# Half of the cross keys kept as differences from the other half: a decoder layer on one NeuronCore

## What is computed

```python
# part 1: linear attention with 16 heads of 64 (relu features)
# part 2, both attentions with 16 heads of 16:
q, k, v = heads(x @ Wq + bq), heads(x @ Wk + bk), heads(x @ Wv + bv)
y = softmax(causal(q @ k.T * scale)) @ v
qc = heads(x @ Wcq + bcq)
kc = heads(context @ Wck + bck)          # 1024 keys
vc = heads(context @ Wcv + bcv)
y = y + softmax(qc @ kc.T * scale) @ vc
x = layernorm(x + y @ Wp + bp)
# part 3: each row goes to the best of 8 experts (256 -> 1024 -> 256)
```

## Time and profile before

| | us |
|---|---|
| median of 3 runs | 2289.46 (2287.99 to 2290.59) |
| the profiled execution | 2287.69 |
| its span in the trace | 2286.0 |
| granted TensorE clock, mean | 0.994 of full speed |

### The profile page before, as it was taken

One profiled execution on the slowest core, in us unless ns is written; L12 is line 12 of the kernel. 1 busy time (PEld: TensorE's weight loads), 2 busy tenths in 40 slices (PEclk: granted clock), 3 DMA queues, 4 the chain that ended last, 5 costly groups with the idle time before them and its releaser, 6 DMA issues. The chain is left out here.

```text
span 2286.0 us, 51067 instructions
## 1 busy us (share of the span) xinstructions
PE 2169.5 (95%) x16290; PEld 1352.2 (59%) x16291; DVE 1366.7 (60%) x3905; ACT 1102.2 (48%) x1680; POOL 367.5 (16%) x628
## 2 busy tenths in 40 slices
PE   8999999999899999999999999999999899799998
PEld 4555554556455555555555645554555455499997
DVE  2588357844785458635883478357844685255554
ACT  1267524761477227732674257524762377233332
POOL 1011111111111111111111111111111111122222
PEclk9999999999999999999999999999999999899999
DMA  7440025102520162005300350026102520655553
GB/s 235 155 164 25 2 106 200 48 2 85 198 71 2 47 234 73 2 11 189 130 25 9 141 180 25 1 97 209 48 2 85 198 71 2 221 181 182 183 182 109
DMA packets 115763, 235.75 MB, mean 103 GB/s; under 512 B 19614, under 2 KB 42655, under 8 KB 113344
## 3 DMA queue, kind: packets, MB, share of 16 engines
q1 hardware_dynamic: 112112, 224.23, 29.3%
q0 software_dynamic: 3408, 8.41, 1.0%
HBM read 154.04 MB, written 73.17 MB: 99 GB/s over the span
## 5 line engine op out<-in xcount | busy, mean ns | idle before, releaser
L1201 ACT ACTIVATE es<-ps 128x1024 f32<-128x1024 f32 (+1 forms) x704 | 665.3, 984 | 250.7 <-PE ps L809 181.4
L1412 DVE TENSOR_REDUCE craw<-ps 128x1 f32<-128x512 f32 x1024 | 636.7, 684 | 115.0 <-PE ps L773 115.0
L773 PE MATMUL ps<-hk,hq 64*128 64x512 f32 x1024 | 391.4, 450 | 24.7 <-DVE craw L1412 8.6
L807 PE MATMUL ps<-hq,hk 64*128 64x512 f32 x1024 | 325.0, 440 | 2.2 <-ACT es L1201 2.2
L1408 DVE CUSTOM_DVE_ANT_0 ps<-ps,causal 128x512 f32<-128x512 f32 (+3 forms) x512 | 236.2, 518 | 91.4 <-PE ps L770 91.0
L773 PEld LDWEIGHTS ps<-hk,hq 64*128 64x128 f32 x1024 | 174.7, 184 | 194.8 <-DVE craw L1412 129.3
L809 PE MATMUL ps<-mrow,minus 64*128 64x512 f32 x1024 | 285.8, 391 | 0.0
L837 PE MATMUL ps<-es,vca 128*17 128x256 f32 x4096 | 276.6, 382 | 1.2 <-ACT es L1201 0.3
L661 POOL TENSOR_SCALAR_AFFINE_SELECT es<-es 128x256 f32<-128x256 f32 x256 | 99.0, 406 | 659.5 <-ACT es L1201 659.4
L1731 ACT ACTIVATE hT<-ph,b1s 128x128 f32<-128x128 f32 x312 | 89.2, 369 | 182.8 <-PE ph L1694 182.8
L809 PEld LDWEIGHTS ps<-mrow,minus 64*128 64x128 f32 x1024 | 166.0, 186 | 10.1
(11 more groups left out here) (210 smaller groups left out, 2838.3 us busy)
## 6 DMA issues: line engine op xcount, KB each, us to landing
w1s<-in_w1T SPq DMA_DIRECT2D x39, 1024.0 KB, 5.4
hk<-scr_kc SPq DMA_DIRECT2D x64, 512.0 KB, 5.1
scr_kc<-staged SPq DMA_DIRECT2D x16, 1024.0 KB, 4.3
scr_qc<-staged SPq DMA_DIRECT2D x32, 512.0 KB, 4.5
scr_q<-staged SPq DMA_DIRECT2D x32, 512.0 KB, 5.3
hq<-scr_qc SPq DMA_DIRECT2D x56, 256.0 KB, 4.4
hq<-scr_q SPq DMA_DIRECT2D x56, 256.0 KB, 4.2
hk<-scr_k SPq DMA_DIRECT2D x56, 256.0 KB, 4.6
```

The source lines that it names most:

```text
L773: last = mm(pb, hq[i][at, T + t * P:T + (t + 1) * P], hk[i][at, T + half * BANK:T + (half + 1) * BANK], start=True, stop=True)
L807: mm(pb[a], hk[i][rows[a], T + j * P:T + (j + 1) * P], hq[i][rows[a], T:2 * T], start=True, stop=False)
L1201: nc.scalar.activation(es[:, k % ERING, :].rearrange("p (a c) -> p a c", a=HB)[:, :, 0:w], eslot[k % 2][:].rearrange("p (a c) -> p a c", a ...
L1412: last = v.reduce_max(craw[p % 2][:, t, a:a + 1, 1 + half], pb, AX.X)
```

## The change

The cross keys of the context's first 512 positions are no longer kept; what stands in their place is their difference from the keys of the last 512 (key i less key i + 512). GpSimd takes the difference of the context itself (context_difference, into a part of es), kcprod multiplies it, and the bias falls out of it. Scores of the first half are then scores of the second half plus the product with the difference, and that product is added onto the bank where the scores of the second half stand:

- exponentials: a unit of the second half is 4 products as before. The unit of the first half two units later goes to the same PSUM tensor, which still holds scores less maximum, and adds 2 products of differences. No maximum is added again.
- maxima: the product for the first half ("rest") is added onto the bank of the second half's, once VectorE has reduced that one. Count and size of products and reductions are the same.

Places in PSUM are worked out anew (places): pair 0 uses four banks for its maxima (zbank is free then), later pairs have bank 1 for the first head and banks 0 and 2 in turn for the second head, the rows and the turned results. The order of maxima (max_of) and of exponential units (UNITS) is by parity of the pair. A step is now: weigh two, 1 maximum, unit k, 1 maximum, unit k+1, 2 maxima (and a row at that border). AHEAD goes from 8 to 12, the first groups from 3 to 4.

```diff
-AHEAD = 8
-ROW_AFTER = (4, 6)
+AHEAD = 12
+ROW_AFTER = (8, 6)
+def cross_tile(c):
+    i = c // 4 * 2 + c % 2
+    return (i, True) if c % 4 >= 2 else (NTC // 2 + i, False)
+OWN_UNITS = [("own", i, False) for i in range(NSELF)]
+CROSS_UNITS = [("cross", *cross_tile(c)) for c in range(NTC)]
+UNITS = (OWN_UNITS + CROSS_UNITS, OWN_UNITS[:2] + CROSS_UNITS + OWN_UNITS[2:])
+SELF_MAX = [("self", i, False) for i in range(len(MAX_SELF))]
+BY_TILE = [("cross", t, rest) for t in range(NT) for rest in (False, True)]
+BY_TWO = [("cross", 2 * n + t, rest) for n in range(NT // 2) for rest in (False, True) for t in range(2)]
+def max_of(p, m):
+    n, a = divmod(m, HB)
+    cross = BY_TWO if a or p == 0 else BY_TILE
+    return (*(cross + SELF_MAX if p % 2 or p == 0 else SELF_MAX + cross)[n], a)
-FIRST_PARTS = [("v", 1, 3), ("qc1", 0, 3), ("q1", 0, 3), ("k1", 0, 3),
+FIRST_PARTS = [("v", 1, 4), ("qc1", 0, 4), ("q1", 0, 4), ("k1", 0, 4),
                ("qf0", 0, 4), ("qf0", 1, 4), ("qf1", 0, 4), ("qf1", 1, 4)]
...
-        order += take(HB)
+        order += take(1)
         if k + 1 < steps:
             order.append(("exp", *divmod(k + 1, NU)))
-        order += take(1)
+        order += take(HB, True)
...
+def places():
+    place, former, last, count = {}, {}, {}, [0, 0]
+    for e in RING:
+        kind, p, m = e
+        if kind == "max" and m % HB == 0:
+            at = (1, 3)[count[0] % 2] if p == 0 else 1
+            count[0] += 1
+        else:
+            at = (0, 2)[count[1] % 2]
+            count[1] += 1
+        place[e], former[e], last[at] = at, last.get(at), e
...
+    return place, former
...
-        eslot = [ps[2], ps[3]]
+        eslot = [ps[3], ps[2]]
...
+            def context_difference():
+                nc.gpsimd.tensor_tensor(ctxd_s, ctxT_s[:, 0:TC_ // 2], ctxT_s[:, TC_ // 2:TC_],
+                                        ALU.subtract).then_inc(s_ctxd, 1)
...
                 first_sum()
+                pool.wait_ge(s_ctx, (b + 2) * 16)
+                context_difference()
                 pool.wait_ge(s_route, b + 1)
...
-                n = RING_AT[entry]
-                if n >= MBANKS:
-                    kind, p, _ = former = RING[n - MBANKS]
+                former = SAME[entry]
+                if former is not None:
+                    kind, p, _ = former
...
-                    last = mm(pb, hq[i][at, T + t * P:T + (t + 1) * P],
-                              hk[i][at, T + half * BANK:T + (half + 1) * BANK], start=True, stop=True)
+                    keys = hk[i][at, T:T + BANK] if rest else hk[i][at, T + BANK:T + TC_]
+                    last = mm(pb, hq[i][at, T + t * P:T + (t + 1) * P], keys, start=not rest, stop=True, skip_group_check=rest)
...
-                if k == 0:
-                    pe.wait_ge(s_act, cur(b, N_ACT, ACT_AT["qf1"]))
+                if k < 2:
+                    pe.wait_ge(s_act, cur(b, N_ACT, ACT_AT[("qf0", "qf1")[k]]))
...
-                turned = range(HB - 1, -1, -1)
+                turned = (0, 1) if k % 2 else (1, 0)
...
                     for a in turned:
-                        mm(pb[a], hk[i][rows[a], T + j * P:T + (j + 1) * P], hq[i][rows[a], T:2 * T], start=True, stop=False)
-                    for a in turned:
-                        last = mm(pb[a], neg[a], mrow[p % 2][rows[a], :], start=False, stop=True)
+                        last = mm(pb[a], hk[i][rows[a], T + j * P:T + (j + 1) * P], hq[i][rows[a], T:2 * T],
+                                  start=not rest, stop=rest, skip_group_check=rest)
+                    if not rest:
+                        for a in turned:
+                            last = mm(pb[a], neg[a], mrow[p % 2][rows[a], :], start=False, stop=True)
...
-                                      ctxT_s[:, half * 512:(half + 1) * 512], start=True, stop=True)
+                                      ctxT_s[:, 512:TC_] if half else ctxd_s, start=True, stop=True)
...
-                    high = nc.scalar.activation(stage[:, stg, 0, at:at + w], t[:, 0:w], ACT.Identity,
+                    skip = TC_ // 2 if w == TC_ else 0
+                    if skip:
+                        nc.scalar.activation(stage[:, stg, 0, at:at + skip], t[:, 0:skip], ACT.Copy)
+                    high = nc.scalar.activation(stage[:, stg, 0, at + skip:at + w], t[:, skip:w], ACT.Identity,
                                                 bias=bias_c[:, bias_n, m:m + 1])
...
-                    for c in range(0, w, 512):
+                    skip = TC_ // 2 if w == TC_ else 0
+                    if skip:
+                        v.tensor_tensor(stage[:, stg, 1, at:at + skip], t[:, 0:skip], stage[:, stg, 0, at:at + skip].bitcast(F32),
+                                        ALU.subtract)
+                    for c in range(skip, w, 512):
```

More of the change, by code:

```diff
@@ L130, in heads_order, with take @@
         maxima.insert(at, ("row", p, 0))
-    def take(count):
+    def take(count, border=False):
         taken = []
-        while maxima and (count or maxima[0][0] == "row"):
+        while maxima and (count or border and maxima[0][0] == "row"):
             count -= maxima[0][0] == "max"
@@ L192 @@
 NEXP = PAIRS * NU
+LAST_IN_Z = max(RED_AT[e] for e in RING if PLACE[e] == 3)
 TILE = 128
@@ L677, in _ @@
                 for kind, p, n in ORDER:
-                    if kind == "exp" and n < NSELF:
-                        cut(p, n)
+                    if kind == "exp" and UNITS[p % 2][n][0] == "own":
+                        cut(p, n, UNITS[p % 2][n][1])
                     elif kind == "turn" and p < PAIRS - 1:
@@ L760, in max_unit @@
                     pe.wait_ge(s_cross[i], b * CROSS[i] + CROSS_AT[p])
-                if (n, a) == (2 * NT, 0):
+                if (what, t, a) == ("self", 0, 0):
                     if p == 0:
@@ L792, in exp_scores @@
                 rows = [slice(a * HROW, (a + 1) * HROW) for a in range(HB)]
-                w = int(n >= NSELF)
+                what, j, rest = UNITS[p % 2][n]
+                w = int(what == "cross")
                 neg = [minus[at, w:w + 1].broadcast_to([HROW, P]) for at in rows]
-                turned = range(HB - 1, -1, -1)
-                if n < NSELF:
-                    for j, col in EXP_SELF[n]:
+                turned = (0, 1) if k % 2 else (1, 0)
+                if what == "own":
+                    for j, col in EXP_SELF[j]:
                         w = T - j * P
@@ L824, in weigh @@
                 z = zbank[:, 0:T // 2] if own else zbank[:, T // 2:T]
-                for j, col in (EXP_SELF[n] if own else [(n - NSELF, 0)]):
+                for j, col in (EXP_SELF[i] if own else [(i, 0)]):
                     first = j if own else 0
@@ L1197, in exp_unit @@
                 def exp_unit(p, n):
-                    w, k = E_COLS[n], p * NU + n
+                    what, i, _ = UNITS[p % 2][n]
+                    w, k = E_COLS[i] if what == "own" else BANK, p * NU + n
                     act.wait_ge(s_sc, cur(b, NEXP, k + 1))
```

69 lines of the change are left out of this document (38 added, 31 removed).

## The result

The changed kernel takes 2295.91 us (median; 2292.01 to 2304.58), the kernel before 2287.72 in the same comparison: ratio 1.0037, interval 1.0027 to 1.0046. It is slower, by 8 us, where I had forecast 40 us faster. The profiled execution has a span of 2294.6 us.

What follows compares the result with a forecast made beforehand. TensorE (2.59 us a step) and VectorE (2.48) were taken as nearly level, tied by the bank. Terms -0.4 - 4.9 + 0.1 + 0.2 = -5.0 us a batch, -40 us, gave 2250 us; range 2216 to 2284.

Steps and rivals of the forecast that it cites:

- groups of four: Maxima before the first exponential: groups of 4 fit the 2.58 us between groups; over 2.6 would show the forecast wrong.
- 8 slots of 0.23: Two pairs' cross exponentials: eight two-product TensorE slots of 0.23 us removed, 1.84 us at most.
- my main claim: Pair loop: most of the 1.84 us two pairs could give stays as a wait for VectorE; 33.24 becomes 32.61.
- The plain step: Cross-maxima step with sixteen weighing products: 1.28 + 0.33 + 0.99 = 2.60 us, against a measured old step of 2.80.
- The restart: Within a step, last maxima slot to start of weighing: 0.33 us.
- Turns and own maxima: Pair loop: step before a turn 3.75 us, turn behind own maxima 3.69, own maxima with row 3.62, one between 2.67.
- The rival "slower": Pair loop: bank 1 turned twice a step without spare; loses above mean step s = 3.11 us, 2315 at 3.20; chance 0.12.
- Ahead of the loop: Before the first exponential unit: added maxima free, later groups wait about as before, one wait gone: -0.4 us a batch.
- The loop: First exponential unit to last maxima step: 35 steps of 2.965 us for 36 of 3.02, -4.9 us a batch.
- The tail: Last maxima step to query features: 18 units for 16, ScalarE the bound, steps of 1.98 us; +0.1 a batch.
- Staging: Cross keys' high part in two ScalarE instructions for one, delaying the query products: +0.2 us a batch.
- The rule against the trace: Steps with maxima: taken strictly, emptying PSUM limits, so removed slots bring nothing; as rival "VectorE unchanged" 2264 us, chance 0.18.

Runs made afterwards that it cites:

- The experiment with the pair dropped in the old layout: The kernel before with 2 of 4 products left out in every second pair of cross exponential units, order and banks unchanged: 2298.35 us, ratio 1.0056.
- the kernel with reductions of 64 columns: The changed kernel with VectorE's cross and own reductions cut to 64 columns: 2170.44 us, ratio 0.9487; the kernel before so cut took 2217.12 us.
- the run with the kept bank: The kernel before with new step order, four banks for pair 0, twelve maxima ahead, and bank 1 only for later pairs' first-head maxima: 2298.18 us, ratio 1.0050.
- the two-part kernel: The kernel before with the new order inside a step, four banks for pair 0 and twelve maxima ahead; all products kept: 2270.05 us, ratio 0.9924.
- the run with products put back: The changed kernel with the minus-maximum products issued again in the cross units that had lost them: 2300.37 us, ratio 1.0059.
- the removal in the best layout: The kernel before with new step order, four banks and twelve maxima ahead, and score products left out in half the cross units: 2271.88 us, ratio 0.9931.
- the run with the new order alone: The kernel before with only the changed order inside a step and of the turned results' halves; ring of three banks and products unchanged: 2281.58 us, ratio 0.9974.

## Why the prediction was wrong, point by point

The step that failed is the comparison of the plain steps. I took the old step as TensorE's own work plus accidental losses, and let the bank's 1.28 us stand only in the new one; it stood in the old one too, so the removal could bring nothing in steps with maxima. Behind that, two costs were too small: the kept bank, laid out for the third maximum alone, cost 28 us in all, and the restart behind a wait and the weighing behind a turn made two pairs 33.91 for the 32.61 laid out. Two of the signs that I had named for being wrong came: two pairs over 33.2, and groups of four over 2.6 us. VectorE's share of 85% and the longer waits of the weight loads came as forecast, and didn't tell a gain from a loss.

**The removed work.** "8 slots of 0.23" was right in number: 512 products fewer; with VectorE's reductions cut short, two pairs differ by 1.36 of the 1.84 us. That only a part would count was my main claim, and it was right in kind: 0.63 us (33.24 to 32.61) for two pairs was still too much. With all else alike the removal brings 0.0 in the new layout (107.76 and 107.79).

**The plain step.** The bank lets the third maximum in at 1.28: right to the hundredth, and the fourth starts with it or 0.09 later. Wrong is the comparison. I took the old step as TensorE's own time, 2.59, stretched by accidents to 2.80, and the slot spacing 0.23 from 1172.45 less 1171.52. But 1172.45 is also 1171.17 + 1.28: the fourth maximum waits for the first one's bank in the old ring just the same, and TensorE's own pace happens to reach it at 1.27. I read the two as one number and not as two limits that stood level. From two limits that stand level, taking away from one gives nothing. The experiment with the pair dropped in the old layout shows it (2.71 for 2.70). Had I put "the last maximum at 1.28" in both columns, the old plain step would have been the same as the new one.

**The restart.** From last slot to weighing I took 0.33, out of the earlier trace rows, where the slots run one behind another. It is 0.32 in the kernel with reductions of 64 columns. Behind a wait it is 0.43 (1605.94 to 1606.37, old layout) to 0.50 (1599.36 to 1599.86), as the first slot of a step costs 0.35 and not 0.23: a slot that has waited is a first slot. This term was mis-sized by 0.10 to 0.18 in four plain steps and in the step before a turn, 0.74 us together, over half of the 1.3 us by which two pairs missed (33.91 for 32.61). The plain steps are 2.69 to 2.78, not 2.60; the two cross steps with fewer or shorter weighing products are 2.55 and 2.57.

**Turns and own maxima.** The step before a turn was put at 3.75 and takes 4.15; the turn behind own maxima at 3.69, and takes 3.94. The twenty weighing products behind a turn take 1.21 now (1606.34 to 1607.55, and 1621.51 to 1622.72). In the kernel before they took 0.99 behind one turn of two pairs (1597.53 to 1598.52) and 1.21 behind the other (1612.63 to 1613.84): the twenty are not of the same units behind every turn. I had carried the cheaper one, the 1.58 of the earlier trace rows, over to both, and that is 0.44 of the 1.3 us. The own step between them, put at 2.67, takes 2.86. The row step (3.20) and the own maxima with their row (3.70 for 3.62) were right.

**The rival that came true.** The rival "slower" named the mechanism that decided: bank 1 turned round twice in each step with no spare. I gave it 0.12, and its price only from s = 3.11 on. It cost 28 us at an s of 3.05 (the run with the kept bank; 3.08 in the changed kernel), because the comparison was not with the old loop but with what the other parts of the change give without it (s = 3.00 with 35 steps). I laid out the kept bank mainly as a wait for the third maximum. Its wait ahead of the loop ("later groups wait for bank 1 about as before") I costed at nothing, and it is 1.6 us a batch; the wait of the next step's first maximum I saw only where few products are weighed, and not as a loss against three banks (2.26 for 2.78). The kept bank as a whole is 3.5 us a batch.

**Ahead of the loop.** Forecast -0.4, measured +0.1 in the last batch (27.21 to 27.28), and at most +0.3 in the others but one (+0.7). The 0.4 for the wait that falls away was right (0.54 in the kernel before). Groups of four were to fit 2.58. They do it every other time:

```profile
1797.14 0.73 PE L828 MATMUL ps<-hk,hq 64*128 64x512 f32 x4 [0.68 <-DMA hq<-staged]
...
1799.73 0.97 PE L828 MATMUL ps<-hk,hq 64*128 64x512 f32 x4
...
1802.54 0.76 PE L828 MATMUL ps<-hk,hq 64*128 64x512 f32 x4
...
1805.14 0.96 PE L828 MATMUL ps<-hk,hq 64*128 64x512 f32 x4
```

2.59, 2.81, 2.60: every second group takes 0.97 for 0.73. Four reductions take 2.48 and leave no slack for the 0.54 in front. The same stands in the two-part kernel, which all the same reaches its first unit 1.2 us sooner; the changed kernel gives that back, as does the run with the kept bank (27.67), where the groups that wait for bank 1 are those of pair 1.

**The loop and the whole.** The loop was forecast at -4.9 a batch and measured at -0.34. The decomposition of the whole time by runs, from the kernel before: order and four banks -16.9 us, kept bank +28.1, the rest of the change (differences, order of units, rows later) +2.2, the removed products -8.3 by the tail's windows, and some +4 at the median, which I put down to the half-clock stretches. The sum is +9; the medians say +8.2. As the last term is the distance from the lowest times to the median, the sum is no test of it.

**The tail.** Forecast +0.1, measured +0.54. I made ScalarE the bound at 1.98. Steps take 2.07, ScalarE idles 0.18, and the second unit's product waits for it:

```profile
1707.40 0.50 PE L861 MATMUL ps<-hq,hk 64*128 64x512 f32 x2
...
1708.05 0.18 PEld L861 LDWEIGHTS ps<-hq,hk 64*128 64x128 f32 x2 [0.35 <-ACT es L1263]
...
1709.47 0.50 PE L861 MATMUL ps<-hq,hk 64*128 64x512 f32 x2
```

**Staging.** Forecast +0.2. The rest of a batch takes 84.64 in both; nothing.

**The rule against the trace.** The Trainium skill, TensorEngine Tiling (Array Packing), section PSUM Bottleneck, has emptying PSUM as the possible limit once TensorE is sped up. Its strict reading, that no slot taken from the steps brings anything, is what the run with products put back shows: 107.76 and 107.79. I argued against it that VectorE is only 83% busy. The share was the wrong row to ask: what binds isn't VectorE's throughput but one bank's way through it, 0.54 + 0.62 + 0.12, and it binds here at a share of 83 to 85%.

## What to carry to other kernels

Before a product is taken away, look which instruction starts the next serial piece of the step, and write down for it both times: when its engine would reach it, and when its buffer is free. If they stand level, as here at 1.27 and 1.28, the removal is worth nothing until the buffer's way is shortened, and the test for it is cheap: shorten the other engine's work and see whether the difference appears. A layout that ties half of the work to one buffer must be paid against the best layout with free rotation, not against the old one: a change of several parts is split into runs, and here two of its parts alone bring 2287 down to 2270, and a third gives it all back and 11 us more.

## What the runs showed of the hardware

TensorE's clock was lower in some kernels with fewer products, and the cause is open. The changed kernel's sixteen runs have a mean granted clock of 0.989 to 0.995; with its products put back all four have 0.994 or 0.995. The old layout with the pair dropped has 0.986 to 0.992, the kernel before 0.994 or 0.995. The traces show it as stretches of 3.4 us at half the clock: four in the loops of the changed kernel (1.2 us dear each), two in the tails of the old layout with the pair dropped (1.5 each). But the removal in the best layout has none in its loops and tails, and the run with the new order alone, from which nothing is removed, has one ahead of its seventh loop (29.04 us for 27.2). The Trainium skill, TensorE: Matmul & The Clock Gate, section A second HAM failure mode: psum-queue depth-cycling, describes a kernel whose TensorE idles briefly between groups as it cycles through PSUM banks, and whose clock goes to and fro for that. This case's trace agrees in what it shows, four stretches at 0.50 behind 2.33 to 2.36 busy of 3.40 us, but no run here shows that these waits are the reason: the kernel with its products put back and the one with the kept bank wait nearly as much for their banks (165.8 and 171.9 us for 198.2) and have no such stretch in their loops.

The two halves of the array can drift apart. Where the two last maxima of a step of the changed kernel don't start together (1.28 and 1.37) the weighing starts 0.07 to 0.08 later, at 1.78 or 1.79 for 1.71 us after the step's first product, and the whole step is that much longer.
